# First routing of a MoE - Mamba - MoE kernel: logits from raw rows, with the gate as TensorE's weights

## The reference

```
x = x + 0.5 * ffn(layernorm(x))        # mixture of experts, first
x = x + attn(layernorm(x))             # Mamba block and an MLP
x = x + 0.5 * ffn(layernorm(x))        # the same experts, second

ffn(h):  logits = h @ gate_w.T + gate_b            # 8 experts
         probs = softmax(logits); take the two largest per token
         each choice has 8 x 640 slots, filled in token order, the rest is dropped
         y += probs_c * (relu(h_e @ W1_e + b1_e) @ W2_e + b2_e)   # FF = 1024
```

## Time and profile before

| | us |
|---|---|
| median of 3 runs (1989.86 to 1990.74) | 1990.0 |
| the profiled execution: its time | 1994.02 |
| the profiled execution: its span in the trace | 1992.2 |
| first routing, up to the barrier | 98.0 |
| of it, from the first normalised rows to the last logits (TensorE) | 19.9 to 60.8 |
| of it, choice of experts (VectorE) | 60.8 to 68.5 |
| of it, table stage | 68.5 to 98.0 |
| mean granted clock of TensorE over the span | 0.931 |

### The profile page before, as it was taken

One profiled execution on the slowest core, in us unless ns is written; L12 is line 12 of the kernel. 1 busy time (PEld: TensorE's weight loads), 2 busy tenths in 40 slices (PEclk: granted clock), 3 DMA queues, 4 the chain that ended last, 5 costly groups with the idle time before them and its releaser, 6 DMA issues. The chain is left out here.

```text
span 1992.2 us, 31078 instructions
## 1 busy us (share of the span) xinstructions
PE 1681.0 (84%) x10860; PEld 1389.6 (70%) x10860; DVE 1615.9 (81%) x2722; ACT 974.2 (49%) x1641; POOL 1290.3 (65%) x799
## 2 busy tenths in 40 slices
PE   6479999996578698888989888998787399999996
PEld 6379999996245465556556555655665299999996
DVE  5657867766469999999999999999997677777675
ACT  1323333332266676676777767676652433333331
POOL 1047646547368888878888887888862356555455
PEclk9989999998779899899989999899888699999998
DMA  6344434442444444445444444445432734344331
GB/s 203 97 116 106 95 78 93 86 80 39 147 139 140 153 137 156 142 135 155 135 151 147 144 155 134 154 138 160 138 112 74 227 75 98 81 91 91 78 69 23
DMA packets 161099, 237.59 MB, mean 119 GB/s; under 512 B 29482, under 2 KB 85408, under 8 KB 160416
## 3 DMA queue, kind: packets, MB, share of 16 engines
q1 hardware_dynamic: 130208, 198.84, 31.9%
q0 software_dynamic: 30720, 36.53, 11.2%
HBM read 202.57 MB, written 38.34 MB: 121 GB/s over the span
## 5 line engine op out<-in xcount | busy, mean ns | idle before, releaser
L1519 POOL TENSOR_TENSOR m_dB<-m_DTU,m_BC 128x1024 f32<-128x1024 f32 x256 | 603.1, 2362 | 153.9 <-DVE m_HS L1615 78.3
L1615 DVE TENSOR_TENSOR_SCAN PS<-PS,m_ST,m_dB 128x512 f32<-128x512 f32 x448 | 552.7, 1271 | 25.8 <-POOL m_dB L1519 25.1
L1272 ACT ACTIVATE PS<-m_DT,m_A 128x512 f32<-128x512 f32 x512 | 332.1, 681 | 195.4 <-DVE m_ST L1631 195.0
L1247 PEld LDWEIGHTS PS<-keep_ident,m_G 128*128 128x128 f32 x2048 | 252.7, 149 | 153.9 <-issue 69.4
L1247 PE MATMUL PS<-keep_ident,m_G 128*128 128x128 f32 x2048 | 292.3, 288 | 56.2 <-POOL m_G L1508 36.4
L1622 DVE TENSOR_TENSOR m_G<-PS,m_BC 128x512 f32<-128x512 f32 x448 | 297.6, 671 | 0.0
L623 PE MATMUL PS<-e_xh,e_wh 128*128 128x256 f32 x1008 | 290.3, 288 | 0.0
L680 ACT ACTIVATE e_hh<-e_u 128x512 fp32r<-128x512 f32 x252 | 156.4, 633 | 270.6 <-DVE e_u L736 267.3
L623 PE MATMUL PS<-e_xl,e_wh 128*128 128x256 f32 x1008 | 284.6, 282 | 0.0
L623 PE MATMUL PS<-e_xh,e_wl 128*128 128x256 f32 x1008 | 284.4, 282 | 0.0
L641 PE MATMUL PS<-e_wh,e_hh 128*128 128x256 f32 x1008 | 281.4, 279 | 0.0
(11 more groups left out here) (245 smaller groups left out, 3021.3 us busy)
## 6 DMA issues: line engine op xcount, KB each, us to landing
m_BC<-bc_rows SPq DMA_DIRECT2D x512, 256.0 KB, 3.8
layer_raw<-w SPq DMA_DIRECT2D x64, 512.0 KB, 3.9
xrows<-r_xn SPq DMA_DIRECT2D x9, 512.0 KB, 4.9
keep_X<-x SPq DMA_DIRECT2D x4, 1024.0 KB, 9.4
sums<-keep_X SPq DMA_DIRECT2D x4, 1024.0 KB, 11.5
out<-keep_X SPq DMA_DIRECT2D x4, 1024.0 KB, 11.2
keep_X<-sums SPq DMA_DIRECT2D x3, 1024.0 KB, 14.7
e_xin<-xrows,e_gix POOLq DMA_INDIRECT x160, 3.2
```

The source lines that it names most:

```text
L1247: last = M(PS[:, B_Y + j, ts], G[:, n % NG, j, ts], C["ident"][:, :], is_transpose=True, start=False, stop=(s == DS - 1 and a == CTT - 1))
L1272: return nc.scalar.activation(out, in_, func, **kw)
L1519: G_.tensor_tensor(dB[:, s % 2, :, :], DTU[:, es, :], BC[:, s % NBC, 0:1, :].to_broadcast([P, 2, CT]), ALU.mult).then_inc(dB_ok, 1)
L1615: V.tensor_tensor_scan(HS[:, :] if on_pool(n, j) else state(n, j), state(n, j), dB[:, s % 2, j, :], ST[:, s, e:e + 1], ALU.mult, ALU.add). ...
```

## The change

1. The four loads of x move from `route` into `setup`, behind the three small loads and before the wait for them. TensorE itself waits for the quarters (`x_in`).
2. TensorE transposes the raw rows of `X`, not the normalised ones. VectorE's norms wait for TensorE no more; the normalised rows are still written and stored.
3. The logits of a group are made turned: the gate's 8 columns are the weights, 512 turned rows are passed through, two products per group, out comes [8, 512]. ScalarE copies this to a new tile `lgT`, and TensorE turns it back with four transposes into PSUM bank 7 (groups 0 to 5) or 6 (groups 6, 7).
4. The three steps are staggered: transposes of group g, product of g - 1, turning back of g - 2.
5. VectorE multiplies the logits by rstd as it reads them from PSUM, adds the bias, and chooses in two calls: 24 tiles, then 8. ScalarE makes the exponentials of both after its last copy.

The diff, cut to its core:

```diff
@@ route, tiles and semaphores
+        lgT = sb("lgT", [EXPERTS, 2, 4 * P])
-        TP0, LG0 = NX, 2
+        back_ok = sem("back_ok")
+        NGR = TT // 4
+        PARTS = [(0, 6, 7), (6, NGR, 6)]
+        def turned_back(g):
+            lo, hi, b = next(part for part in PARTS if part[0] <= g < part[1])
+            return PS[:, b, (g - lo) * 4 * EXPERTS:(g - lo + 1) * 4 * EXPERTS]
@@ SyncE
-                for q in range(4):
-                    sp.dma_start(X[:, q * Q:(q + 1) * Q, :], ...).then_inc(x_in[q], 16)
@@ VectorE
-                    dve.wait_ge(tp_ok, h * NX + (g + 1))
-                dve.wait_ge(lg_ok, TT // 4 + LG0)
-                link(V.tensor_tensor(lg[:, :, :], lg[:, :, :], C["gb"]..., ALU.add))
-                choose(V, dve, link, C, dict(lg=lg, pr=pr, w1=w1, red=red), slice(0, TT), sh_ok, ex_ok, 1)
+                dve.wait_ge(rstd_ok, QUARTERS)
+                for call, (lo, hi, b) in enumerate(PARTS):
+                    ts, n = slice(4 * lo, 4 * hi), 4 * (hi - lo)
+                    dve.wait_ge(back_ok, hi)
+                    link(V.tensor_tensor(lg[:, ts, :], PS[:, b, 0:n * EXPERTS].rearrange("p (t e) -> p t e", e=EXPERTS),
+                                         rstd[:, ts].unsqueeze(2).to_broadcast([P, n, EXPERTS]), ALU.mult))
+                    link(V.tensor_tensor(lg[:, ts, :], lg[:, ts, :], C["gb"]..., ALU.add))
+                    choose(V, dve, link, C, dict(lg=lg, pr=pr, w1=w1, red=red), ts, sh_ok, ex_ok, call + 1)
@@ ScalarE
+                for g in range(NGR + 1):
+                    if g < NGR:
+                        act.wait_ge(tp_ok, g + 1)
+                        if g >= 2:
+                            act.wait_ge(lgp_ok, g - 1)
+                        nc.scalar.activation(xnT[:, g % 2, :, :], PS[:, 2 * (g % 2):2 * (g % 2) + 2, :], ACT.Copy).then_inc(xnT_ok, 1)
+                    if g >= 1:
+                        act.wait_ge(lgp_ok, g)
+                        if g >= 3:
+                            act.wait_ge(back_ok, g - 2)
+                        nc.scalar.activation(lgT[:, (g - 1) % 2, :], PS[0:EXPERTS, 4 + (g - 1) % 2, :], ACT.Copy).then_inc(lg_ok, 1)
+                for call, (lo, hi, b) in enumerate(PARTS):
+                    act.wait_ge(sh_ok, call + 1)
+                    nc.scalar.activation(lg[:, 4 * lo:4 * hi, :], lg[:, 4 * lo:4 * hi, :], ACT.Exp).then_inc(ex_ok, 1)
@@ TensorE
-            pe.sem_inc(tp_ok, TP0)
-            pe.sem_inc(lg_ok, LG0)
+            for g in range(NGR + 2 if x_dram is not None else 0):
+                if g < NGR:
+                    pe.wait_ge(x_in[g // 2], 16)
+                    if g >= 2:
+                        pe.wait_ge(xnT_ok, g - 1)
+                    for k in range(DK):
+                        for a in range(4):
+                            last = nc.tensor.transpose(PS[:, 2 * (g % 2) + k, a * P:(a + 1) * P], X[:, 4 * g + a, k * P:(k + 1) * P],
+                                                       C["ident"][:, :])
+                    last.then_inc(tp_ok, 1)
+                if 1 <= g <= NGR:
+                    pe.wait_ge(xnT_ok, g)
+                    if g == 1:
+                        pe.wait_ge(centred, 1)
+                    if g >= 3:
+                        pe.wait_ge(lg_ok, g - 2)
+                    for k in range(DK):
+                        last = nc.tensor.matmul(PS[0:EXPERTS, 4 + (g - 1) % 2, :], C["gate"][:, k, :], xnT[:, (g - 1) % 2, k, :],
+                                                start=(k == 0), stop=(k == DK - 1))
+                    last.then_inc(lgp_ok, 1)
+                if g >= 2:
+                    pe.wait_ge(lg_ok, g - 1)
+                    for a in range(4):
+                        last = nc.tensor.transpose(turned_back(g - 2)[:, a * EXPERTS:(a + 1) * EXPERTS], lgT[:, g % 2, a * P:(a + 1) * P],
+                                                   C["ident"][0:EXPERTS, 0:EXPERTS])
+                    last.then_inc(back_ok, 1)
@@ setup, SyncE, after the loads of the gate, its bias and b1
+            for q in range(4):
+                rows = TOKENS // 4
+                sp.dma_start(X[:, q * (TT // 4):(q + 1) * (TT // 4), :],
+                             x[q * rows:(q + 1) * rows, :].rearrange("(t p) d -> p t d", p=P)).then_inc(sem_maker(nc, C, "r0")(f"x_in{q}"), 16)
             sp.wait_ge(loaded, 48)
```

More of the change, by code:

```diff
@@ L170, in _ @@
         def _(sp):
-            if x_dram is not None:
-                for q in range(4):
-                    sp.dma_start(X[:, q * Q:(q + 1) * Q, :],
-                                 x_dram[q * Q * P:(q + 1) * Q * P, :].rearrange("(t p) d -> p t d", p=P)).then_inc(x_in[q], 16)
             def store(h):
@@ L259, in norm @@
                     last.then_inc(xn_ok, 1)
-            bc = lambda a: a.unsqueeze(2).to_broadcast([P, TT, EXPERTS])
             if x_dram is not None:
@@ L268, in _ @@
                     norm(h, 1)
-                dve.wait_ge(lg_ok, TT // 4 + LG0)
-                link(V.tensor_tensor(lg[:, :, :], lg[:, :, :], C["gb"][:, :].unsqueeze(1).to_broadcast([P, TT, EXPERTS]), ALU.add))
-                choose(V, dve, link, C, dict(lg=lg, pr=pr, w1=w1, red=red), slice(0, TT), sh_ok, ex_ok, 1)
+                dve.wait_ge(rstd_ok, QUARTERS)
[4 more added lines that the diff above has]
+                                         rstd[:, ts].unsqueeze(2).to_broadcast([P, n, EXPERTS]), ALU.mult))
+                    link(V.tensor_tensor(lg[:, ts, :], lg[:, ts, :], C["gb"][:, :].unsqueeze(1).to_broadcast([P, n, EXPERTS]), ALU.add))
+                    choose(V, dve, link, C, dict(lg=lg, pr=pr, w1=w1, red=red), ts, sh_ok, ex_ok, call + 1)
             for c in range(TOPK):
@@ L391, in _ @@
                 last.then_inc(mean_ok, 1)
[L392 to L404, removed]
-                        for a in range(4):
[L406 to L410, removed]
@@ L1727, in build @@
         sums = nc.dram_tensor("sums", (TOKENS, D), FP32, kind="Internal").ap()
-        setup(nc, C, gate, gate_b, b1)
+        setup(nc, C, gate, gate_b, b1, X, x)
         tokens_to_experts(nc, "0", X, C, PS, xrows, sums, w1, w2, b2, x)
@@ L1758, in _, with setup @@
                     start = n
-def setup(nc, C, gate, gate_b, b1):
+def setup(nc, C, gate, gate_b, b1, X, x):
     ctx = ExitStack()
```

## The result

The changed kernel took 1973.72 us (median of 6 runs, 1969.30 to 1975.14), the kernel before beside it 1989.93 us (6 runs, 1983.99 to 1990.74). The ratio is 0.9938, its 95% interval 0.9916 to 0.9959: faster by 0.6%, between 8 and 17 us (the two medians are 16.2 us apart, inside this interval at its far end). Two later sets of runs gave 0.9927 (0.9904 to 0.9950) and 0.9920 (0.9892 to 0.9949). The forecast was 1971.3, and the range 1968 to 1978.

What follows compares the result with a forecast made beforehand. TensorE was taken to bound the routing from 19.9 to 60.6 us, then VectorE. The compare moves from 68.5 to 49.8, -18.7 us, taking the 1990.0 median to 1971.3; range 1968 to 1978.

Steps and rivals of the forecast that it cites:

- The x loads: Setup block: issues of 5.68 us open the barrier at 8.3, 3.9 us later; VectorE loses 0.6 us.
- TensorE's start and group: Gate pass: first transpose at 9.7, eight groups of 3.05 us at full clock, end 36.9 plus about 0.8.
- The clock: New gate pass: 5.5 us at 1.2 GHz before the clock rises, costing 2.8 us; transposes taken to count as activity.
- The row: Profile evidence cited: from 1434.13 to 1438.43 transposes alone, 20 at 0.22 us, then four at the full-clock value.
- Rival 2: Gate pass: TensorE stays at 1.2 GHz, gain only 1.3 us, total 1988.7; chance 0.05.
- VectorE late next: After the norms VectorE is the bound: choice starts at 38.2 instead of 60.8, takes 11.6, compare at 49.8.
- The stores: Routing's end: weights' store lands at 69 to 70, before the barrier at 79.3; 9 us left, so covered.
- rivals 3 and 4: Setup wait lasts until x lands, 1979 or 1996.5 (0.02); gain given back later, up to 10 us, 1981 (0.04).
- The table stage: From the one-hot compare to 98 us: no change, since it starts with a cold TensorE before and after.
- The prediction's sign: Test for being wrong: the shift at the one-hot compare, forecast as 18.7 us, is not that of the end.
- the base of the sum: Old gate pass: clock never rose, four pairs made 40.7 us at 1.2 GHz, compare at 68.5.

Runs made afterwards that it cites:

- x_in_route: The changed kernel with the four loads of x back in the routing block, as before; 1972.55 us, ratio to the kernel before 0.9936.
- before_2, before_1: The kernel before, unedited, run again for another trace; it and the other such rerun took 1981.7 and 1981.9 us.
- one_call: The changed kernel with one choice of 32 tiles in place of 24 and 8; 1969.24 us, ratio to the kernel before 0.9922.
- warm: Changed kernel with one choice and two x loads in setup, plus 32 idle products in both expert stages; 1966.13 us against 1966.75 without them.
- normed: The changed kernel's new product and turning back, but from normalised rows, without VectorE's factor 1/std; 1983.34 us, ratio to the kernel before 1.0003.
- dense: The kernel before plus two unread 128x128 by 512-column products after each pair's transposes; 1988.61 us against 1989.62, ratio 1.0011.

## Why the prediction was right, and where it was not

- **The x loads.** Barrier foreseen at 8.3, was 8.55; statistics at 10.8, were 11.09. The issues took 5.90 instead of 5.68. Right; x_in_route confirms the sign, a loss of 0.3 to 0.7.
- **TensorE's start and group.** First transpose 9.7, was 9.82. A group at the full clock 3.05, was 3.18: transposes 1.03 instead of 0.9, the product 1.81 instead of 1.72 (so weights of 8 columns were not cheaper than those of 128), turning back 0.34 instead of 0.43. The end 37.7, was 37.25. That it came so close is in part luck: eight groups cost 1.0 us more than counted, and the low clock cost about 1.3 us less.
- **The clock.** I took 5.5 us of low clock and 0.86 us per record until about 16. It rose sooner: the product at 13.41 has the full pace, behind 3.6 us of transposes and, ahead of these, 0.9 us of the 8-column products of L397. In two more traces of the changed kernel it rose within the first product.
  In the Trainium skill, "TensorE: Matmul & The Clock Gate", Part 4, transposes don't count for the clock. The traces speak against it. The row has 3.3 us of 8-column products right ahead of its transposes (L1201, from 1430.86), so it and the changed kernel's first group are no clean cases, but the first burst of before_2 is one: 14.1 us of standing, 16 transposes, the full pace. Rival 2, that TensorE stays low in the new pass, is out in all three traces.
- **VectorE late next.** Choice from 38.2, was 38.30; 11.6 long, was 11.61; compare 49.8, was 49.91. The step on which the sum rests held to 0.1 us, and one_call shows that VectorE was the bound. The compare moved by 18.6 us, 18.7 were forecast.
- **The stores.** Landing of the weights' store at 69 to 70 with 9 us left; it landed at about 67.4 and SyncE stood 12.4. Covered. With the barrier at 8.55, and the first gather 17.9 us sooner, rivals 3 and 4 are out too.
- **The table stage** I took as untouched. It grew by 0.7 us: VectorE waits 3.64 us for the end of the table (L434, bracket at 77.99) instead of the 2.91 in the trace of before, because the granted clock was 0.50 in all of 50 to 80, where in the trace of before the last rounds of that stage ran at the full pace. A small term that was missing. The prediction's sign, that the shift at the compare is that of the end, can't be read from one pair of executions: it is 18.6 at the compare, 17.9 at the first gather and 22.3 at the end of the two traces.
- **Where it failed: the base of the sum.** "The old stage alternated ... and never rose" was read from one execution and taken for the kernel. In before_2 it rose in four pairs, in before_1 in three. The routing ends at 99.2, 91.0 and 86.9 in the three traces of before, and at 81.4 in the changed one: the gain is 17.9, 9.6 or 5.5 us, by the execution that it is compared with. The 18.7 of the forecast is right for the first kind alone. The forecast met the time (1971.3 against 1973.7) because base and gain belong together: by its times the base of 1990.0 is of that kind too, and the changed kernel's time doesn't depend on the kind. The change itself is smaller than forecast: 12 us by the ratio, 16.2 by the medians, and at most 17 by the interval. Two of the six executions of before took 1984.0 and 1984.7 us, and a base that mixes both kinds explains the sign of this; how much of it, no trace of those six shows. Rival 2 weighed the same uncertainty for the new pass and never for the old one.

## What to carry to other kernels

Ask which engine is late next before you split its work: here the split of the choice was meant to overlap with an engine that had become the faster one, and cost 3.5 us. DMA issues placed ahead of a barrier's wait are paid by all engines: here two of 1 MB held it for 0.3 us and four for 4.1, so measure how long the issues take before you put them there. And take the base of a forecast from more than one execution when a stage's price follows the clock: the old gate pass ran 28 or 41 us in the same program.

## What the hardware showed that was not expected

- The granted clock reads 1.00 in 20 to 60 us of the profiled execution of before while the records there have twice the duration they have later (0.213 against 0.106 us for 8 columns passed). The column can't be trusted ahead of its first change.
- Bursts of 16 fp32 transposes, 3.1 to 3.5 us long, were followed by the full clock in before_2 in all of four, in before_1 in three of four, in the trace shown ahead in none of four. The first burst of each stands behind 14 us of idle time, the others behind 8-column products.
- The clock is lost in a wait of 3.2 us (warm) and of 2.2 us (normed), and also behind 3.7 us of unbroken 8-column products (before_2).
- Products with 8 columns of weights and 512 passed have nearly the pace of full ones: 1.81 us for four records, against 1.72 with 128 columns of weights (dense, L403). Turning back from 8 partitions takes 0.34 us for four.
